# Attention on one core: row sums of the second query tile taken by ScalarE, and the late weighting cut in two

## What is computed

```python
b, t, d = x.shape                                   # 8, 512, 1024, after a layer norm
q = (x @ wq_w.T + wq_b).reshape(b, t, H, HD)        # 32 heads of 32
k = (x @ wk_w.T + wk_b).reshape(b, t, HKV, HD)      # one head of keys and values
v = (x @ wv_w.T + wv_b).reshape(b, t, HKV, HD)
...
scores = jnp.einsum('bqhd,bkd->bhqk', q, k1) / jnp.sqrt(jnp.float32(HD))
scores = jnp.where(causal, scores, -jnp.inf)
weights = jax.nn.softmax(scores, axis=-1)
attn = jnp.einsum('bhqk,bkd->bqhd', weights, v1)
attn = attn.reshape(b, t, H * HD)
return attn @ wo_w.T + wo_b
```

## Time and profile before

| what | value |
|---|---|
| time, median of 3 runs | 3011.81 us (3009.79 to 3011.86) |
| the profiled execution, its own time | 3019.18 us |
| its span from first to last instruction | 3017.4 us |
| granted TensorE clock, mean | 0.957 |
| busy share of the span | PE 92%, DVE 53%, ACT 39%, POOL 31% |
| attention | about the first 1700 us |

### The profile page before, as it was taken

The page is one execution under the profiler, slowest core; times in us unless marked ns, Lnnn a source line. Parts: engine busy times, 40 slices in busy tenths (PEclk is TensorE's granted clock), DMA queues, the critical chain, the costliest instruction groups (busy, mean ns, idle before and its releaser), DMA issues. The chain is left out here.

```text
span 3017.4 us, 41859 instructions
## 1 busy us (share of the span) xinstructions
PE 2789.1 (92%) x15808; PEld 2121.5 (70%) x15808; DVE 1612.7 (53%) x2960; ACT 1168.2 (39%) x2509; POOL 949.2 (31%) x1460
## 2 busy tenths in 40 slices
PE   4888999999999999999999987999999999999988
PEld 3566767767677677676775565777878787878766
DVE  3453464553644645536435256666666666676653
ACT  2664365453653644536546012222222222222220
POOL 2433122121221221212212134535353535354422
PEclk9889999999999999999998978999999999999989
DMA  5765544544545445445444520010202020202011
GB/s 153 196 162 155 163 106 147 125 110 127 127 104 164 108 143 128 109 130 126 109 140 130 169 75 1 1 57 1 56 1 57 1 56 1 56 1 56 1 29 28
DMA packets 103626, 272.29 MB, mean 90 GB/s; under 512 B 12122, under 2 KB 23514, under 8 KB 101122
## 3 DMA queue, kind: packets, MB, share of 16 engines
q1 hardware_dynamic: 102706, 269.55, 32.9%
q10 hardware_dynamic: 720, 0.07, 0.0%
HBM read 168.40 MB, written 50.33 MB: 72 GB/s over the span
## 5 line engine op out<-in xcount | busy, mean ns | idle before, releaser
L645 DVE TENSOR_REDUCE top<-ps_attn 128x1 fp32r<-128x512 f32 (+3 forms) x704 | 438.7, 634 | 488.4 <-PE ps_attn L817 487.6
L455 POOL TENSOR_SCALAR_AFFINE_SELECT pt<-pt 128x512 f32<-128x512 f32 x256 | 163.9, 651 | 945.3 <-ACT pt L542 945.3
L556 ACT ACTIVATE spent<-ps_attn,top 128x512 f32<-128x512 f32 (+1 forms) x512 | 325.7, 636 | 260.3 <-DVE top L645 258.9
L1532 PE MATMUL ps_mixer<-m_w_hi,m_xt_hi 128*128 128x512 f32 x1024 | 422.4, 413 | 1.6 <-DVE m_xt_lo L1314 1.6
L542 ACT ACTIVATE pt<-ps_attn 128x512 f32<-128x512 f32 (+1 forms) x704 | 379.7, 557 | 100.7 <-PE ps_attn L844 100.1
L1533 PE MATMUL ps_mixer<-m_w_hi,m_xt_lo 128*128 128x512 f32 x1024 | 407.8, 398 | 0.0
L1534 PE MATMUL ps_mixer<-m_w_lo,m_xt_hi 128*128 128x512 f32 x1024 | 406.9, 397 | 0.0
L814 PE MATMUL ps_attn<-k_stack,q_stack 96*128 96x512 f32 (+3 forms) x1024 | 302.4, 347 | 46.7 <-ACT spent L556 30.1
L844 PE MATMUL ps_attn<-q_stack,k_stack 97*128 97x512 f32 (+3 forms) x1024 | 294.1, 347 | 29.3 <-DMA q_stack<-top_rows 22.8
L1214 ACT CAST m_xt_hi<-ps_mixer 128x512 fp32r<-128x512 f32 x192 | 104.3, 590 | 494.1 <-PE ps_mixer L1527 494.0
L814 PEld LDWEIGHTS ps_attn<-k_stack,q_stack 96*128 96x128 f32 x1024 | 173.5, 193 | 113.5 <-ACT spent L556 55.3
(11 more groups left out here) (216 smaller groups left out, 5127.9 us busy)
## 6 DMA issues: line engine op xcount, KB each, us to landing
xr<-in_a_x SPq DMA_DIRECT2D x64, 512.0 KB, 6.5
q_stack<-q_hi SPq DMA_DIRECT2D x128, 256.0 KB, 5.6
wq_hi<-wq_split SPq DMA_DIRECT2D x56, 512.0 KB, 4.0
wq_lo<-wq_split SPq DMA_DIRECT2D x56, 512.0 KB, 4.6
q_stack<-q_lo SPq DMA_DIRECT2D x64, 256.0 KB, 6.8
wo_hi<-wo_split SPq DMA_DIRECT2D x8, 2048.0 KB, 8.3
wo_lo<-wo_split SPq DMA_DIRECT2D x8, 2048.0 KB, 13.0
x<-xr SPq DMA_DIRECT2D x32, 512.0 KB, 2.8
```

The lines of the kernel that those rows point to most:

```text
L556: nc.scalar.activation(spent[:, 0:width], ps[:, S0 + n % 2, 0:width], ACT.Exp, scale=-1.0, bias=top[:, j * TILES + i:j * TILES + i + 1].bi ...
L645: nc.vector.tensor_reduce(out, ps[:, S0 + n % 2, 0:width * len(heads)].rearrange("p (j k) -> p j k", k=width), AX.X, ALU.min).then_inc(s_u ...
L1532: nc.tensor.matmul(out, a_hi, b_hi, start=first, stop=False)
```

## The change

`SUM_TILES` goes from 2 to 3. ScalarE makes row sums for query tile 1 too: units 8 and 9, two heads each, one instruction of 256 columns for each head. The ones products shrink from 256 to 128 columns in `weigh_first` and vanish from `weigh_second`, which transposes three tiles in place of two. One of the two reciprocals goes, and `take_inverse` copies 384 columns. `den_invert` moves behind `divide`. `weigh_rest` is cut: tile 2 stands after unit 5, tile 3 after unit 7.

```diff
-    SUMMED, SUM_TILES = 8, 2
+    SUM_TILES = 3
+    SUMS = [len(heads) if i >= TILES - SUM_TILES else 0 for i, heads in S_UNITS]
+    SUMMED = sum(SUMS)
     SUM_COL = (T // P - SUM_TILES) * P
...
                 def row_sum(G, u):
-                    if u >= SUMMED:
+                    if u >= U:
                         return
-                    i, (j,) = S_UNITS[u]
+                    i, heads = S_UNITS[u]
                     n = U * G + u
                     width = (i + 1) * P
...
+                    for m, j in enumerate(heads if SUMS[u] else ()):
+                        ahead = SUMMED * G + sum(SUMS[:u]) + m
+                        act.wait_ge(s_used, n + 1)
+                        if u == 0 and G:
+                            act.wait_ge(den_inv_done, G)
+                        if ahead:
+                            act.wait_ge(den_done, ahead)
+                        nc.scalar.activation(spent[:, 0:width], ps[:, S0 + n % 2, m * width:(m + 1) * width], ACT.Exp, scale=-1.0,
+                                             bias=top[:, j * TILES + i:j * TILES + i + 1].bitcast(F32),
+                                             accum_out=den[:, i - (TILES - SUM_TILES), j:j + 1]).then_inc(den_done, 1)
...
-                def invert(G, part):
...
-                    cols = slice(part * P, (part + 1) * P)
-                    nc.vector.reciprocal(att[:, G % 2, cols], ps[:, DEN, cols]).then_inc(inv_done, 1)
+                    nc.vector.reciprocal(att[:, G % 2, 0:SUM_COL], ps[:, DEN, 0:SUM_COL]).then_inc(inv_done, 1)
...
                     if inside(M - 1):
-                        invert(M - 1, 1)
                         take_inverse(M - 1)
                     if first is not None:
                         x_low(first, 0)
                     if inside(M + 1):
                         tops(M + 1, (9, 10))
-                        den_invert(M + 1)
                     if first is not None:
                         x_low(first, 1)
                     if inside(M - 1):
                         divide(M - 1)
+                    if inside(M + 1):
+                        den_invert(M + 1)
...
                         if held:
-                            pe.wait_ge(den_done, (n - 2) // U * SUMMED + (n - 2) % U + 1)
+                            pe.wait_ge(den_done, (n - 2) // U * SUMMED + sum(SUMS[:(n - 2) % U + 1]))
...
-                def weigh_rest(G):
+                def weigh_third(G):
+                    pe.wait_ge(sel_done, TILES * G + 3)
+                    weigh(G, 2)
+
+                def weigh_fourth(G):
                     pe.wait_ge(sel_done, TILES * (G + 1))
-                    weigh(G, 2)
                     weigh(G, 3).then_inc(b_done, 1)
...
-                        if u == 4 and inside(M - 1):
-                            weigh_rest(M - 1)
+                        if u == 5 and inside(M - 1):
+                            weigh_third(M - 1)
+                        if u == 7 and inside(M - 1):
+                            weigh_fourth(M - 1)
```

More of the change, by code:

```diff
@@ L180, in attention_blocks @@
         ident_r, causal_r = sb("ident_r", [P, P], F32R), sb("causal_r", [P, P], F32R)
-        spent, den, den_inv = sb("spent", [P, T]), sb("den", [P, 2, GH]), sb("den_inv", [P, 2, 2, GH])
+        spent, den, den_inv = sb("spent", [P, T]), sb("den", [P, SUM_TILES, GH]), sb("den_inv", [P, 2, SUM_TILES, GH])
         identb_sb, causal_sb = spent[:, 0:P // 2].bitcast(BF16), spent[:, P // 2:P].bitcast(BF16)
@@ L545, in row_sum @@
                 def row_sum(G, u):
-                    if u >= SUMMED:
+                    if u >= U:
                         return
-                    i, (j,) = S_UNITS[u]
+                    i, heads = S_UNITS[u]
                     n = U * G + u
                     width = (i + 1) * P
-                    act.wait_ge(s_used, n + 1)
-                    if u == 0 and G:
-                        act.wait_ge(den_inv_done, G)
-                    if u or G:
-                        act.wait_ge(den_done, SUMMED * G + u)
-                    nc.scalar.activation(spent[:, 0:width], ps[:, S0 + n % 2, 0:width], ACT.Exp, scale=-1.0,
-                                         bias=top[:, j * TILES + i:j * TILES + i + 1].bitcast(F32),
-                                         accum_out=den[:, i - (TILES - SUM_TILES), j:j + 1]).then_inc(den_done, 1)
+                    for m, j in enumerate(heads if SUMS[u] else ()):
[8 more added lines that the diff above has]
+                                             accum_out=den[:, i - (TILES - SUM_TILES), j:j + 1]).then_inc(den_done, 1)
                 def q_high(G):
@@ L646, in tops, with invert @@
                                                 AX.X, ALU.min).then_inc(s_used, 1)
-                def invert(G, part):
-                    if part == 0:
-                        dve.wait_ge(b_done, 2 * G + 1)
-                        if G >= 2:
-                            dve.wait_ge(olo_done, G - 1)
-                    cols = slice(part * P, (part + 1) * P)
-                    nc.vector.reciprocal(att[:, G % 2, cols], ps[:, DEN, cols]).then_inc(inv_done, 1)
+                def invert(G):
+                    dve.wait_ge(b_done, 2 * G + 1)
+                    if G >= 2:
+                        dve.wait_ge(olo_done, G - 1)
+                    nc.vector.reciprocal(att[:, G % 2, 0:SUM_COL], ps[:, DEN, 0:SUM_COL]).then_inc(inv_done, 1)
                 def take_inverse(G):
@@ L666, in divide @@
                     dve.wait_ge(b_done, 2 * (G + 1))
-                    dve.wait_ge(inv_done, 3 * (G + 1))
+                    dve.wait_ge(inv_done, 2 * (G + 1))
                     nc.vector.tensor_tensor(att[:, G % 2, :], ps[:, AV, :], att[:, G % 2, :], ALU.mult).then_inc(att_done, 1)
@@ L717, in _ @@
                     if inside(M - 1):
-                        invert(M - 1, 0)
+                        invert(M - 1)
                     if inside(M + 1):
```

## The result

| | before | after |
|---|---|---|
| time, median of 4 runs | 3011.84 us (3009.79 to 3014.82) | **3129.52 us** (3126.48 to 3138.32) |
| the profiled execution, its own time | 3019.18 us | 3127.93 us |
| its span | 3017.4 us | 3126.1 us |
| granted TensorE clock, mean | 0.957 | 0.939 |

The ratio after to before is 1.039, with a 95% interval of 1.037 to 1.041. The changed kernel is slower by 118 us. The forecast was slower by 64, with 3112 as the upper end of its range, so its direction holds, its size is off, and the time lies outside the range.

What follows compares the result with a forecast made beforehand. TensorE was taken to bound a plain step's front, and hand-overs between TensorE, VectorE and ScalarE its end. 3012 us plus 41 for steps and longer ends plus 23 for clock falls gave 3076 us, range 3010 to 3112.

Steps and rivals of the forecast that it cites:

- a plain step ends up 0.1 to 0.2 us longer: Plain steps: an end about 0.9 us longer nearly cancels against savings at the front and turn; 30 x 0.15 = 5 us.
- the 23 us for the clock: Plain and output steps: TensorE's clock falls in a third of 44, at 1.6 us each; bounds none and 70 us.
- The bound: Plain step: TensorE bounds the front; in the end TensorE, VectorE and ScalarE hand units over, where the new ScalarE work goes.
- the second rival: TensorE is the bound after all; the pairs vanish in ScalarE's 5 us spare: 18 us saved, 2994; chance 0.10 for a gain.
- The price of a row sum: ScalarE: a 256 column row sum lasts 0.47 us, its read starts at 0.37; a pair takes 1.06 (0.85 to 1.3).
- What TensorE gets back: TensorE ahead of unit 4: 0.25 + 0.33 saved on ones products, 0.10 for a third transpose, so 0.48 us.
- The new end and the turn: Plain step: the projection chunk starts about 0.9 us later; the turn gives most back, as nobody waits for tops 10 and division.
- The cut weighting: Tiles 2 and 3 weighted in two pieces: costed at nothing where TensorE waits anyway, 0.2 us a step without that cover.
- first batch, steps 0 to 7: ScalarE's split of wo comes behind the second pair: 1.5 us for each of five steps, 2.4 in step 5; 10 us.
- 14 output steps: Steps 0 and 1 of batches 1 to 7: output projection hides the turn, 14 x 0.9 = 13 us, plus 2 for DMA waits.
- step 5, six batches: Batches 1 to 6: the x halves, VectorE's parts and the pairs queue behind each other; 1.3 x 6 = 8 us.
- the clock falls in nearly every step: Rival: longer ends plus a clock fall in nearly every step, 41 + 70 = 111 us, 3123; chance 0.06.

Runs made afterwards that it cites:

- x5: The changed kernel without ScalarE's row sums of query tile 1, which are read as a constant 1 (result not the reference's): 2979.5 us, ratio 0.990.
- x2: The kernel before with only the cut late weighting and the reciprocal of the sums behind the division; SUM_TILES stays 2: 2991.3 us, ratio 0.994.
- x11: The kernel before with only the cut weighting and the moved reciprocal, measured a second time: 2997.7 us, ratio 0.995.
- x1: The changed kernel with the weighting of tiles 2 and 3 put back in one piece after unit 4: 3190.7 us, ratio 1.060.
- x4: The changed kernel plus three unused products of constants ahead of turned unit 10, in steps that transpose no x: 3090.6 us, ratio 1.027.
- x6: The changed kernel with a pair's second row sum written to the other half of `spent`, so no wait inside a pair: 3075.2 us, ratio 1.023.

## Why the prediction was right in kind and wrong in size

Two terms of the sum failed. The first is the step "a plain step ends up 0.1 to 0.2 us longer": at the full clock it is 0.63 longer. The second is the 23 us for the clock: it cost about 42 in the plain and output steps. The mechanism behind both, a longer end and falls of the clock behind it, is the one that was forecast.

**The bound, right.** The end of a plain step is a hand-over between engines, and new ScalarE work put there lengthens it. x5 against after (150 us) shows it, and the second rival, TensorE as the bound after all, is refuted: its own conditions failed, since a pair took 1.12 us and not 0.6.

**The price of a row sum, right.** 256 columns took so long in 196 instructions of the changed kernel from 400 to 1700 us (busy, mean ns; idle before):

```profile
L560 ACT ACTIVATE spent<-ps_attn,top 128x256 f32<-128x256 f32 x196 | 93.0, 475 | 28.2 <-DVE top L649 13.9
```

The estimate was 0.47. The accumulator read starts 0.37 to 0.38 behind it, as estimated. The second sum of a pair starts 0.09 behind the read's end (852.90 to 852.99), where I had put 0.04, so a pair is 1.12 for 1.06, and 0.12 a step come from there.

**What TensorE gets back, too large.** I took 0.48 us. By the timelines the first weighting shrank from 1.43 (from 771.81 to 773.24) to 1.22, and the second with its transposes from 1.20 (781.13 to 782.33 in the trace of before) to 1.09: three transposes cost more than I allowed. Together 0.32, and x5 against x2 has 0.31. The row sum of unit 6 starts 11.60 behind the first weighting (850.21 - 838.61), where it was 11.81 and should have been 11.33. Of the two, the term that was off is the 0.23 saved at the second weighting, which measured 0.11. Another 0.11 went at turned unit 0: it takes 0.34 us until the next product (842.01 to 842.35) where it took 0.23 before (775.42 to 775.65). It waits for the DMA of `top_rows`, which SyncE issues at 839.14 and which lands 2.8 us later. Step 36 of the changed kernel, where that DMA lands sooner, does not have it, so this part belongs to step 28 and not to every step.

**The new end and the turn, too small.** Turned unit 10 was to come 16.4 behind the first weighting. It came 855.59 - 838.61 = 16.98 behind it. The 0.6 are the 0.27 above, the 0.12 of the pairs, and a gap ahead of the first pair: exp 6 (851.71) leaves ScalarE free at about 852.1, and the pair starts at 852.34, since VectorE reduces tops 8 only from 851.61 on, behind its reciprocal. I had put 0.04 there. Behind turned unit 10 all went as forecast (0.50 until the projection, the wait of 0.80, none for VectorE). So the failed step is "a plain step ends up 0.1 to 0.2 us longer": it is 0.63 (18.35 for 17.72, third and fourth step of a batch). Errors of 0.1 to 0.3 in the terms became four times the result, since that result was the small difference of large ones.

**The cut weighting, mispriced by itself.** I costed it at nothing as hidden. Its earlier score units stood in my new end, but I never asked what they are worth alone: 0.67 us in two steps of a batch and 14 to 19 us in all (x11, x2), 61 in the changed kernel (x1). So the direction of each half escaped me: one half gains, the other loses far more than the sum shows.

**The clock, right in kind, too small.** The shortest falls cost what I took from the earlier trace rows: step 16, the first output step of its batch, is 42.15 us with one and 40.56 at the full clock (in x4), 1.6. But I put a fall in a third of the 44 plain and output steps. In steps 8 to 61, which are 42 of them, 22 falls begin after and one before. Nine of them also last longer, as that of step 26 does over the turn to step 27: together the clock stands low for 102 us there in place of 10, 4.7 us for each fall. x4, with its products in the wait before turned unit 10, has 4 such falls left, so most of them follow that wait.

**By places**, in the profiled executions, from transpose of the tops to transpose of the tops:

| steps | forecast | measured |
|---|---|---|
| first batch, steps 0 to 7 | +10 | +12 |
| 14 output steps | +15, and 7 of clock | +30 |
| 29 plain steps | +5, and 16 of clock | +46 |
| step 5, six batches | +8 | +12 |
| step 6 | +3 | +9 |

These add up to 109 us, which is the difference of the two spans (the kernel before took 7 us more in its profiled execution than in its median; hence 118 between medians). The windows go from turn to turn, so what an end loses and what the next turn gives back can stand in two rows: at the full clock the third and fourth steps of a batch are 0.63 longer, but the second and seventh 1.2 (18.4 for 17.2), the first output step 0.8 and the second 1.3. Each step taken at its length at full clock, the plain steps account for some 24 us and the output steps for some 10. The rest of both, 76 - 34 = 42 us, is clock, where 23 were forecast; half of the 92 us of low clock more is 46, which is the most that it can be. So of the 45 us that are missing against the forecast of 64, about 19 are clock, 14 are ends, and 12 are in steps 5, 6 and the first batch, where I did not separate the two. The rival "the clock falls in nearly every step" gives almost the measured time (3123), but by the wrong sum: with shorter ends and more falls than there were.

## What to carry to other kernels

Where engines hand units to each other, price work by its place in the chain, not by the idle share of the engine that gets it: here 2.2 us a step on an engine that idled for 5 cost 1.6 us a step. Price each half of a compound change by itself, since the sum of this one hid a half that gains 14 to 19 us. And when a sum of large terms comes out near zero, carry the error of the terms into the range; each new wait on TensorE also puts its clock at risk, beyond its own length.

## What the runs showed of the hardware

- With waits of 0.3 and 0.8 us, two to a step, 22 falls to 0.50 begin in 42 plain and output steps, where one did before, and three products without use (0.85 us) in the longer wait left 4 of them. Over the attention the falls went from 44 to 21, and the time from 3129.5 to 3090.6 us.
- The same waits did not come with a fall each time. The end of step 42 has the waits of 0.32 and 0.80 too, and its window of TensorE (length, busy, instructions, clock, DMA) shows the full clock with 28% idle, as do those behind it:

```profile
1244.00:1248.00 4.00, 2.88 (x17) 1.00 0.46 55
1248.00:1252.00 4.00, 4.00 (x32) 1.00 0.27 87
```

  So the share of ends with a fall can be counted, but no row here tells which end falls.
- Within ScalarE, an instruction that waits for the semaphore raised by the one before it started 0.09 us after that one's end; with a second buffer in its place (x6) the second sum of a pair started 0.46 after the first instead of 0.65.
